# A two-layer transformer block on one core: q and k parts stored part-major and gathered in runs of neighbouring rows, and the first row maxima issued earlier

## The chip, the cores and the metric

The kernel runs on one NeuronCore of one Trainium2 chip. The metric is device microseconds of one launch. The kernel before has a median of 708.69 us over three runs (708.49, 708.69 and 711.36).

## The reference, cut to what matters

One sequence of 1024 tokens with 256 features passes two layers. Each layer has adaptive layer norms, an attention and an MLP, joined by gated residual updates.

Layer 0: a chunked linear attention with rotary embedding, then a gated MLP with 4-bit weights (2048 hidden features). Layer 1: causal softmax attention with 16 heads of 16 features and rotary embedding, then a second causal softmax attention of the same shape (no rotary embedding) inside the MLP branch, whose result modulates a gated MLP with 1024 hidden features.

```python
# layer 1, first attention (the second has no _rope and no biases)
q = _rope(proj(Wq, bq)); k = _rope(proj(Wk, bk)); v = proj(Wv, bv)
att = einsum('bhqd,bhkd->bhqk', q, k) / sqrt(16)
att = softmax(where(causal, att, -inf))
y = einsum('bhqk,bhkd->bhqd', att, v) @ Wo.T + bo
```

The change touches only the two softmax attentions, called "the first" (`l = 0` in `attention(l)`) and "the second" (`l = 1`) below.

## The kernel before, in words

The program is written out by engine; semaphores order the engines. TensorE computes projections, scores and products; VectorE and ScalarE move results out of PSUM; GpSimd (POOL) does small subtractions; the SP queue issues all DMAs.

Scores need more precision than bf16 gives, at bf16 speed. So q and k are each split in three bf16 parts (high, middle, low), and one matmul contracts over 96 rows: 16 features times six products of parts. For that, q and k stand in SBUF tiles `qr` and `kr`, [row, half of the tokens, head, token], where row 6*d + slot holds feature d of the part that belongs to the slot. Rows 96 to 98 of `qr` hold the row maxima, in three bf16 parts, and those of `kr` hold -1, so that a score comes out with its row maximum already subtracted.

The way of q and k in each attention: the projection lands feature-major in PSUM (in the first attention by way of rotary embedding on token-major tiles, L1179 to L1203, and transposes on TensorE, L697). `split` (ScalarE L923 to L940, VectorE L1216 to L1230, POOL `low_parts` L1611 to L1617) makes the three parts in pieces of 128 features by 512 tokens: `w` 0 to 3 are q and k of features 0 to 127 and 128 to 255 of the first token half, 4 to 7 those of the second half. `parts_out` (L395) stores a q piece and a k piece to a DRAM scratch `scr`, 384 KB each, and `spread` (L403) gathers them back with twelve DMAs of 128 KB, one for each slot of `qr` and of `kr`; it waits for both stores. The landing of one `spread(l, half, dt)` is counted in `qr_ld{2*half+dt}`.

Then the attention. There are eight blocks: four groups of four heads, for the first half of the queries (c = 0) and then for the second (c = 1). For each block there are banks of the row maxima (`max`: matmuls L742, mask L745, VectorE's maximum L1285), a `rowmax` step (POOL splits the maxima in three parts, TensorE transposes them at L751, ScalarE copies them to `m3T` at L973, and SP's `row_max` at L414 puts them into `qr` by a DMA), then per tile of 128 keys the scores (L768, mask L771), the exponential (ScalarE L962) and the product with v (L782). TensorE walks a list `ORDER`, computed once before the build by `attention_order()` from assumed costs; the same list serves both attentions, and ScalarE and VectorE walk it too. It starts with eleven banks of block 0, five of block 1, `rowmax` of block 0, six more banks of block 1, the first bank of block 2, and then the first score of block 0. Ahead of that first score TensorE runs six matmuls whose result nobody reads (`idle(6, 4)`, L760, executed at L471), and waits for the -1 rows and for the row maxima of block 0. A ring of three PSUM banks serves the maxima. In the second attention ScalarE waits ahead of the exponentials of the second step until the last stores of the second token half have landed (L956), since the tile `pt` shares memory with their source.

The order on the SP queue is written out at L421 to L434: store and gather of the first two pieces, then of the next two, the first store of the second half (`parts_out(l, 1, 0)`), `row_max(l, 0)`, the other store of the second half, its gathers and the other row maxima.

Of the kernel before, what the change touches and what calls it, by code (L numbers as in the profile page):

```python
# [186 lines left out]
def build(nc, a, out):  # L187
# [13 lines left out]
    with ctx:  # L201
# [59 lines left out]
        def piece(l, n, half):  # L261
# [54 lines left out]
        scr = nc.dram_tensor("parts_scratch", [4, P, 3, T], BF16, kind="Internal").ap()  # L316
# [10 lines left out]
            qt sp_h sp_r sp_m sp_l sp_p pw0 pw1 pw2 pw3 qr_ld0 qr_ld1 qr_ld2 qr_ld3 vp_e  # L327
# [3 lines left out]
            dq w_sc wf_h wf_l g_m u_m gl_s it_s it_h it_l fdn out_done""".split()  # L331
        names += [f"nat{i}" for i in range(FC[1])] + [f"ld_scale{i}" for i in range(4)]
# [10 lines left out]
        def _(sp):  # L343
# [77 lines left out]
            for l in range(2):  # L421
                parts_out(l, 0, 0)
                spread(l, 0, 0)
                parts_out(l, 0, 1)
                spread(l, 0, 1)
                parts_out(l, 1, 0)
                row_max(l, 0)
                parts_out(l, 1, 1)
                spread(l, 1, 0)
                row_max(l, 1)  # L430
                row_max(l, 2)
                spread(l, 1, 1)
                for blk in range(3, len(BLOCKS)):
                    row_max(l, blk)  # L434
# [15 lines left out]
        def _(pe):  # L450
# [260 lines left out]
            def attention(l):  # L711
# [19 lines left out]
                for what, i, *at in ORDER:  # L731
                    if what == "max":
                        blk, g, c, qt, ch, w, h0, k = BANKS[i]
                        if (g // 2, c) not in loaded:
                            loaded.append((g // 2, c))
                            pe.wait_ge(S[f"qr_ld{2 * c + g // 2}"], 16 * 12 * (l + 1))
# [17 lines left out]
                    elif what == "score":  # L754
# [111 lines left out]
        def _(act):  # L866
            def weight_hi(i, dst, off):
                if i == 0:
                    act.wait_ge(S["ld_raw0"], 80)
                elif i == 5:  # L870
                    act.wait_ge(S["ld_raw1"], 64)
                    act.wait_ge(S["vj"], 8)
                elif i == 9:
                    act.wait_ge(S["ld_raw2"], 64)
                    act.wait_ge(S["pw1"], 32)
                    act.wait_ge(S["pw3"], 32)
# [46 lines left out]
            def split(l, first=0, last=8):  # L923
                def middle(w):
                    act.wait_ge(S["sp_r"], 8 * l + w + 1)
                    half, n = divmod(w, 4)
                    act.copy(piece(l, n, half)[:, (1, 2)[n % 2], :], rest[:, w % 4, :]
                             ).then_inc(S["sp_m"], 1)

                for w in range(first, last + 1):  # L930
                    if w < last:
                        half, n = divmod(w, 4)
                        act.wait_ge(S["qt"], 8 * l + w + 1)
                        if l == 1 and w == 0:
                            for i in range(4):
                                act.wait_ge(S[f"pw{i}"], 32)
                        act.copy(piece(l, n, half)[:, (0, 1)[n % 2], :], bank[w % 4][:, :]
# [10 lines left out]
            def attention(l):  # L948
                act.activation(sd[:, 0:1], minus1[:, :], ACT.Exp)
                for what, i, *at in ORDER:  # L950
                    if what == "score":
# [3 lines left out]
                        if l == 1 and i == 1 and at[0] == 0:  # L955
                            act.wait_ge(S["pw3"], 64)  # L956
# [135 lines left out]
        def _(ve_):  # L1092
# [80 lines left out]
            def pairs(ap, l, i):  # L1173
# [3 lines left out]
                return ap.rearrange("p (h two j) -> p h two j", h=2 * H, two=2)[:, :, i, :]  # L1177

            def rope_cos(l, t):  # L1179
                dve.wait_ge(S["pj"], 8 * l + t + 1)  # L1180
                if t >= 2:
                    dve.wait_ge(S["rp_add"], 8 * l + t - 1)
                dve.tensor_tensor(t1[:, t % 2, :].rearrange("p (h d) -> p h d", d=DH),
                                  bank[4 + 2 * (t % 2)][:, :].rearrange("p (h d) -> p h d", d=DH),
                                  rope_c[:, l, t, :].unsqueeze(1).to_broadcast([P, 2 * H, DH]), ALU.mult
                                  ).then_inc(S["rp_t1"], 1)

            def rope_sin(l, t):
# [3 lines left out]
                for i in range(2):  # L1192
                    z = pairs(t2[:, t % 2, :], l, i), pairs(bank[4 + 2 * (t % 2)][:, :], l, 1 - i)
                    s = rope_s[:, l, t, :].rearrange("p (j two) -> p two j" if l == 0 else "p (two j) -> p two j", two=2)[:, i, :]
                    q = dve.tensor_tensor(z[0], z[1], s.unsqueeze(1).to_broadcast([P, 2 * H, DH // 2]), ALU.mult)
# [20 lines left out]
            def split(l, first=0, last=8):  # L1216
                for w in range(first, last + 1):
                    if w < last:
                        half, n = divmod(w, 4)
                        dve.wait_ge(S["sp_h"], 8 * l + w + 1)  # L1220
                        if w >= 4:
                            dve.wait_ge(*low_part(l, w - 4))
                        dve.tensor_tensor(rest[:, w % 4, :], bank[w % 4][:, :],
                                          piece(l, n, half)[:, (0, 1)[n % 2], :], ALU.subtract
                                          ).then_inc(S["sp_r"], 1)
                    if first < w <= 2:
# [3 lines left out]
                                          piece(l, n, half)[:, (1, 2)[n % 2], :], ALU.subtract).then_inc(S["sp_l"], 1)  # L1230
# [19 lines left out]
            def low_rank_halves():  # L1250
# [7 lines left out]
                for i in range(4):  # L1258
                    dve.wait_ge(S[f"pw{i}"], 64)
# [257 lines left out]
        def _(pool):  # L1517
# [93 lines left out]
            def low_parts(l):  # L1611

                for w in range(2, 8):
# [3 lines left out]
                                       piece(l, n, half)[:, (1, 2)[n % 2], :], ALU.subtract).then_inc(S["sp_p"], 1)  # L1617
# [83 lines left out]
```

## Time and profile before

| | |
|---|---|
| median of three runs | 708.69 us |
| profiled execution | 708.0 us |
| its span, first to last instruction | 706.1 us |
| TensorE busy | 654.3 us (93%) |
| VectorE busy | 457.2 us (65%) |
| ScalarE busy | 334.4 us (47%) |
| POOL busy | 149.7 us (21%) |
| mean granted TensorE clock | 0.988 of full |
| gathers into `qr` and `kr` | 96 DMAs of 128 KB |
| stores to the scratch | 16 DMAs of 384 KB |

Busy times of TensorE overlap with each other at their ends, because matmuls are pipelined. All dates in the rows are microseconds from the start of the span. The first attention begins its row maxima at 289.41, the second at 478.14.

### The profile page before, as it was taken

To read this page: it belongs to the slowest core of one execution; us is meant where nothing else is said; L and a number is where in the kernel's file an instruction comes from. 1 tells how busy PE (TensorE), PEld (TensorE's weight loads), DVE (VectorE), ACT (ScalarE), POOL (GpSimd) and SP (SyncE) were. 2 spreads that over 40 slices of the span, in tenths; PEclk is the share of its full clock that TensorE was granted. 3 is DMA by queue.
4 is the path that set the end of the run, shared out by engine and by line. 5 is a ranking of instruction groups with operands and counts; after the bars stand their busy time and mean duration, and the time that the engine had idled before them with its cause. 6 is when DMAs were issued, how large, how long until landed. Compare 5 with 4: busy or idle time off the path is not lost.

```text
span 706.1 us, 10697 instructions
## 1 busy us (share of the span) xinstructions
PE 654.3 (93%) x3990; PEld 405.8 (57%) x3990; DVE 457.2 (65%) x970; ACT 334.4 (47%) x531; POOL 149.7 (21%) x194
## 2 busy tenths in 40 slices
PE   4999979999999879899999998897999999999996
PEld 3667647777777656455444434483554444368884
DVE  5668787777777388778888602557788886242223
ACT  5334243333333423345567684561564657843332
POOL 3002224555555601310000000031100001003331
PEclk9999799999999999999999999999999999999999
DMA  7602410000000002663000000037410000050001
GB/s 263 227 0 91 128 44 0 24 23 22 1 0 1 0 1 75 190 186 92 2 2 2 1 2 1 1 125 227 137 54 2 2 2 2 20 160 1 1 0 59
DMA packets 36415, 38.34 MB, mean 54 GB/s; under 512 B 4034, under 2 KB 35292, under 8 KB 36108
## 3 DMA queue, kind: packets, MB, share of 16 engines
q1 hardware_dynamic: 36364, 37.67, 17.0%
q8 instruction: 31, 0.51, 0.3%
q14 instruction: 20, 0.16, 0.1%
HBM read 30.11 MB, written 7.34 MB: 53 GB/s over the span
## 4 chain that ended last, share of the span: by engine, by line
PE 47%; issue 22%; POOL 12%; DVE 11%; ACT 3%; DMA 2%; SPq 2%; POOLq 0%; DVEq 0%; ACTq 0%
POOL it_lo L1602 9%; PE psum L782 9%; PE psum L742 8%; PE psum L768 8%; PE psum L454 4%; DVE m L1285 3%; PE psum L455 3%; PE psum L456 3%; POOL wd L1581 2%; PE psum L771 2%; PE psum L745 2%; PE psum L471 2%; PE psum L570 1%; DVE mx L1285 1%; SPq L345 1%
## 5 line engine op out<-in xcount | busy, mean ns | idle before, releaser
L962 ACT ACTIVATE pt<-psum 128x1024 f32<-128x1024 f32 (+1 forms) x192 | 148.1, 811 | 93.2 <-PE psum L771 65.1
L1285 DVE TENSOR_REDUCE mx<-psum 128x1 f32<-128x512 f32 (+3 forms) x216 | 132.4, 665 | 16.3 <-PE psum L742 8.3
L742 PE MATMUL psum<-kr,qr 96*128 96x512 bf16 (+3 forms) x384 | 108.6, 332 | 5.7 <-DVE m L1285 2.7
L768 PE MATMUL psum<-qr,kr 99*128 99x512 bf16 (+3 forms) x384 | 97.6, 327 | 1.5 <-ACT pt L962 1.3
L1602 POOL TENSOR_TENSOR it_lo<-it,it_hi 128x512 fp32r<-128x512 f32 x48 | 67.3, 1402 | 146.2 <-ACT it_hi L1006 144.6
L782 PE MATMUL psum<-pt,vp 128*32 128x512 f32 (+3 forms) x768 | 81.7, 498 | 0.0
L454 PE MATMUL psum<-h_hi,wf_hi 128*128 128x512 f32 x192 | 75.4, 393 | 1.7 <-issue 1.7
L742 PEld LDWEIGHTS psum<-kr,qr 96*128 96x128 bf16 x384 | 36.3, 98 | 68.0 <-DVE mx L1285 29.4
L1006 ACT CAST it_hi<-it 128x512 fp32r<-128x512 f32 x48 | 29.9, 623 | 95.7 <-DVE it L1360 95.7
L455 PE MATMUL psum<-h_lo,wf_hi 128*128 128x512 f32 x192 | 74.8, 390 | 0.0
L456 PE MATMUL psum<-h_hi,wf_lo 128*128 128x512 f32 x192 | 74.8, 389 | 0.0
L1285 DVE TENSOR_REDUCE m<-psum 128x1 f32<-128x384 f32 (+3 forms) x88 | 50.6, 636 | 20.2 <-PE psum L745 19.9
L1360 DVE TENSOR_TENSOR it<-psum,gl 128x512 f32<-128x512 f32 x48 | 32.9, 685 | 43.0 <-PE psum L456 39.7
L768 PEld LDWEIGHTS psum<-qr,kr 99*128 99x128 bf16 x384 | 35.4, 98 | 41.3 <-ACT pt L962 23.0
L771 PE MATMUL psum<-identb,tri 128*128 128x128 bf16 x256 | 50.3, 219 | 0.0
L745 PE MATMUL psum<-tri,identb 128*128 128x128 bf16 x256 | 50.2, 224 | 0.0
L1630 POOL TENSOR_SCALAR m<-m 128x16 bf16<-128x16 f32 x16 | 4.1, 254 | 213.1 <-DVE m L1289 153.9
L454 PE MATMUL psum<-it_hi,wf_hi 128*128 128x512 f32 x96 | 39.4, 411 | 7.3 <-POOL it_lo L1602 7.3
L454 PEld LDWEIGHTS psum<-h_hi,wf_hi 128*128 128x128 f32 x192 | 36.1, 188 | 10.2 <-issue 2.5
L455 PEld LDWEIGHTS psum<-h_lo,wf_hi 128*128 128x128 f32 x192 | 36.1, 188 | 7.8 <-issue 0.2
L456 PEld LDWEIGHTS psum<-h_hi,wf_lo 128*128 128x128 f32 x192 | 36.0, 188 | 7.7
L1002 ACT ACTIVATE gl<-psum 128x512 f32<-128x512 f32 x48 | 28.6, 596 | 24.6 <-PE psum L533 16.4
(201 smaller groups left out, 1087.1 us busy)
## 6 DMA issues: line engine op xcount, KB each, us to landing
qr<-parts_scratch SPq DMA_DIRECT2D x48, 128.0 KB, 2.7
kr<-parts_scratch SPq DMA_DIRECT2D x48, 128.0 KB, 2.6
parts_scratch<-parts SPq DMA_DIRECT2D x12, 384.0 KB, 3.2
wmod<-in_L_wmod SPq DMA_DIRECT2D x1, 1536.0 KB, 6.3
parts_scratch<-qr SPq DMA_DIRECT2D x4, 384.0 KB, 3.2
x<-in_L_attn_x SPq DMA_DIRECT2D x2, 512.0 KB, 4.3
wmod<-in_L_wmod SPq DMA_DIRECT2D x1, 1024.0 KB, 5.3
packed<-in_L_ffn_gate_W_packed SPq DMA_DIRECT2D x1, 1024.0 KB, 7.2
```

The source lines that it names most:

```text
L454: pe.matmul(dst, st_hi, mv_hi, start=first, stop=False)
L455: pe.matmul(dst, st_hi, mv_lo, start=False, stop=False)
L456: return pe.matmul(dst, st_lo, mv_hi, start=False, stop=last)
L742: m = pe.matmul(b, qr[0:PARTS_ROWS, c, h, (qt - 4 * c) * P:(qt - 4 * c + 1) * P], kr[0:PARTS_ROWS, ch, h, 0:w], start=True, stop=not diag)
L745: m = pe.matmul(b[:, w - P:w], identb[:, :], tri[:, :], start=False, stop=True)
L768: m = pe.matmul(bank[4 + 2 * at[0] + j][:, 0:w], kr[0:PARTS_ROWS + 3, kt // 4, h, (kt % 4) * P:(kt % 4 + 1) * P], qr[0:PARTS_ROWS + 3, c, ...
L771: m = pe.matmul(bank[4 + 2 * at[0] + j][:, 0:P], tri[:, :], identb[:, :], start=False, stop=True)
L782: m = pe.matmul(bank[3][32 * j:32 * j + 32, q0 - c * HALF:q0 - c * HALF + w], vp[:, kt, 4 * gp + j, :], pt[:, (n + j // 2) % 4, j % 2, 0:w ...
L962: act.activation(pt[:, n % 4, :, 0:w], psum[:, b:b + 2, 0:w], ACT.Exp, scale=0.25).then_inc(S["ex"], 1)
L1285: dve.tensor_reduce(dst, bank[at[0]][:, 0:k * w].rearrange("p (k w) -> p k w", k=k), AX, ALU.max).then_inc(S["p1_mx"], 1)
L1360: dve.tensor_tensor(it[:, N % 2, :], bank[5][:, :], gl[:, N % 2, :], ALU.mult).then_inc(S["it_s"], 1)
L1602: pool.tensor_tensor(it_lo[:, N % 2, :], it[:, N % 2, :], it_hi[:, N % 2, :].bitcast(F32), ALU.subtract).then_inc(S["it_l"], 1)
```

## The change

1. The scratch is [4, part, 128 features, tokens] instead of [4, 128 features, part, tokens].
2. Within each 128 features, q and k are ordered by feature and then by head (d, h) instead of (h, d). For that, the columns of the weights and the biases of q and k of both attentions are permuted on the host, and the rotary embedding of the first attention multiplies with a table that is repeated over eight heads along the innermost axis.
3. The parts of k are kept in the opposite order from q's (q high, middle, low; k low, middle, high). The 96 rows are now 16 * slot + feature, and the six products need, for q, parts 0, 1, 2, then 0, 1, then 0, and for k, parts 0, 1, 2, then 1, 2, then 2 of its own order. So each gathers with three DMAs, of 48, 32 and 16 rows, 384, 256 and 128 KB.
4. The stores of q and k have their own semaphores; the gathers of q wait for q's store alone.
5. `row_max(l, 0)` stands ahead of `parts_out(l, 1, 0)` on the SP queue.
6. The six idle matmuls ahead of the first score are gone.

```diff
-        scr = nc.dram_tensor("parts_scratch", [4, P, 3, T], BF16, kind="Internal").ap()
+        scr = nc.dram_tensor("parts_scratch", [4, 3, P, T], BF16, kind="Internal").ap()
...
-                    sp.dma_start(scr[w2, :, :, tok], piece(l, w2, half)).then_inc(S[f"pw{2 * half + dt}"], 16)
+                    sp.dma_start(scr[w2, :, :, tok].rearrange("s p t -> p s t"), piece(l, w2, half)).then_inc(S[f"{'qk'[is_k]}w{2 * half + dt}"], 16)
...
-                sp.wait_ge(S[f"pw{2 * half + dt}"], 32 * (l + 1))
-                for is_k, (dst, order) in enumerate([(qr, (0, 1, 0, 1, 0, 2)), (kr, (1, 1, 2, 2, 0, 1))]):
-                    for slot, part in enumerate(order):
-                        sp.dma_start(dst[slot:PARTS_ROWS:6, half, 8 * dt:8 * dt + 8, :],
-                                     scr[2 * dt + is_k, :, part, tok].rearrange("(h d) t -> d h t", d=DH)
+                for is_k, dst in enumerate((qr, kr)):
+                    sp.wait_ge(S[f"{'qk'[is_k]}w{2 * half + dt}"], 16 * (l + 1))
+                    for first, part, n in ((0, 0, 3), (3, is_k, 2), (5, 2 * is_k, 1)):
+                        src = scr[2 * dt + is_k, part:part + n].rearrange("s (d h) t -> (s d) h t", d=DH)
+                        sp.dma_start(dst[DH * first:DH * (first + n), half, 8 * dt:8 * dt + 8, :], src[:, :, tok]
                                      ).then_inc(S[f"qr_ld{2 * half + dt}"], 16)
...
+                row_max(l, 0)
                 parts_out(l, 1, 0)
-                row_max(l, 0)
                 parts_out(l, 1, 1)
...
-                            pe.wait_ge(S[f"qr_ld{2 * c + g // 2}"], 16 * 12 * (l + 1))
+                            pe.wait_ge(S[f"qr_ld{2 * c + g // 2}"], 16 * 6 * (l + 1))
...
                             if blk == 0:
-                                idle(6, 4)
                                 pe.wait_ge(S["kr_ones"], 4)
...
-                return ap.rearrange("p (h two j) -> p h two j", h=2 * H, two=2)[:, :, i, :]
+                return ap.rearrange("p (g two j h) -> p g two j h", g=4, two=2, h=8)[:, :, i, :, :]
...
+                    z = [v.rearrange("p (g d h) -> p g d h", g=4, h=8) for v in (t1[:, t % 2, :], bank[4 + 2 * (t % 2)][:, :])]
+                    c = rope_c[:, l, t, :].unsqueeze(1).unsqueeze(3).to_broadcast([P, 4, DH, 8])
...
+                        s = s.unsqueeze(1).unsqueeze(3).to_broadcast([P, 4, DH // 2, 8])
```

The rest of the diff follows from these: the indices of the parts in `split`, the waits that named the old store semaphores (L875, L876, L936, L956, L1259), and the permutations on the host.

## Rows read from the trace of the kernel before

**Rows 1.** The page's clock line: 40 slices of 17.65 us, in tenths of full speed.
```profile
PEclk9999799999999999999999999999999999999999
```

**Rows 2.** Windows: stretch, us, busy time (instructions) by engine, clock, DMA share, GB/s.
```profile
303.00:325.00 22.00, 22.00 (x198) 11.70 (x197) 16.28 (x30) 11.70 (x20) 2.38 (x11) 1.00 0.57 168
478.00:479.00 1.00, 0.86 (x13) 0.87 (x14) 0.20 (x1) 0.99 (x2) 0.00 (x0) 1.00 1.04 358
493.00:494.00 1.00, 1.00 (x4) 0.41 (x3) 0.00 (x0) 0.00 (x0) 0.00 (x0) 0.51 1.00 350
```

**Rows 3.** TensorE's timeline, first attention: start, us, engine, line, operation, count, idle before.
```profile
287.67 1.90 PE L471 MATMUL psum<-spin,identb 128*128 128x512 bf16 x8 [1.02 <-DVE xn L1223]
289.41 0.22 PE L742 MATMUL psum<-kr,qr 96*128 96x128 bf16 x1
...
302.13 1.81 PE L471 MATMUL psum<-spin,identb 128*128 128x512 bf16 x6
303.78 0.38 PE L768 MATMUL psum<-qr,kr 99*128 99x512 bf16 x1
```

**Rows 4.** Waits, 289 to 320 and then 477 to 510 us: total, times, longest.
```profile
PEld psum L742 <- DMA kr<-parts_scratch: 0.5, 1, 0.5
...
PE psum L742 <- DMA kr<-parts_scratch: 0.9, 1, 0.9
```

**Rows 5.** TensorE's timeline, second attention.
```profile
478.14 0.22 PE L742 MATMUL psum<-kr,qr 96*128 96x128 bf16 x1 [0.93 <-DMA kr<-parts_scratch]
...
490.52 0.27 PE L742 MATMUL psum<-kr,qr 96*128 96x128 bf16 x1 [0.71 <-DVE m L1285]
...
491.33 2.77 PE L471 MATMUL psum<-spin,identb 128*128 128x512 bf16 x6
493.89 0.43 PE L768 MATMUL psum<-qr,kr 99*128 99x512 bf16 x1
```

**Rows 6.** Timeline of the SP queue, second attention.
```profile
464.11 1.94 SPq L401 DMA_DIRECT2D parts_scratch<-parts  x2
...
484.09 4.43 SPq L410 DMA_DIRECT2D kr<-parts_scratch  x6
...
489.88 0.79 SPq L418 DMA_DIRECT2D qr<-m3T  x1
490.71 1.57 SPq L401 DMA_DIRECT2D parts_scratch<-parts  x2
```

**Rows 7.** The page's DMA issues: count, KB each, median us from issue to landing.
```profile
kr<-parts_scratch SPq DMA_DIRECT2D x48, 128.0 KB, 2.6
parts_scratch<-parts SPq DMA_DIRECT2D x12, 384.0 KB, 3.2
```

**Rows 8.** VectorE's timeline at 489 us.
```profile
489.22 1.28 DVE L1285 TENSOR_REDUCE m<-psum 128x1 f32<-128x512 f32 x2
```

**Rows 9.** Timeline of the SP queue, first attention.
```profile
295.15 3.81 SPq L410 DMA_DIRECT2D kr<-parts_scratch  x6
...
300.32 0.83 SPq L418 DMA_DIRECT2D qr<-m3T  x1
```

**Rows 10.** ScalarE's timeline, both attentions.
```profile
298.41 0.26 ACT L973 COPY m3T<-psum 48x128 bf16<-48x128 bf16 x1 [8.62 <-PE psum L751]
...
477.24 0.37 ACT L920 COPY vp<-psum 128x256 f32<-128x256 f32 x1 [0.34 <-PE psum L456]
...
487.13 0.26 ACT L973 COPY m3T<-psum 48x128 bf16<-48x128 bf16 x1 [8.00 <-PE psum L751]
494.69 1.02 ACT L962 ACTIVATE pt<-psum 128x1024 f32<-128x1024 f32 x1 [7.30 <-PE psum L771]
```

**Rows 11.** VectorE's groups by form up to 460 us: count, busy us, mean ns, idle before.
```profile
L1195 DVE TENSOR_TENSOR t<-psum,rope_s 128x256 f32<-128x256 f32 x32 | 12.0, 416 | 0.2
L1183 DVE TENSOR_TENSOR t<-psum,rope_c 128x512 f32<-128x512 f32 x16 | 11.0, 686 | 15.8 <-PE psum L482 15.8
L1415 DVE TENSOR_TENSOR xn<-psum,rc 128x256 f32<-128x256 f32 x8 | 3.4, 419 | 0.0
```

More of the change, by code:

```diff
@@ L331, in build @@
             dq w_sc wf_h wf_l g_m u_m gl_s it_s it_h it_l fdn out_done""".split()
+        names += [f"{z}w{i}" for z in "qk" for i in range(4)]
         names += [f"nat{i}" for i in range(FC[1])] + [f"ld_scale{i}" for i in range(4)]
@@ L926, in middle @@
                     half, n = divmod(w, 4)
-                    act.copy(piece(l, n, half)[:, (1, 2)[n % 2], :], rest[:, w % 4, :]
+                    act.copy(piece(l, n, half)[:, 1, :], rest[:, w % 4, :]
                              ).then_inc(S["sp_m"], 1)
@@ L935, in split @@
                             for i in range(4):
-                                act.wait_ge(S[f"pw{i}"], 32)
-                        act.copy(piece(l, n, half)[:, (0, 1)[n % 2], :], bank[w % 4][:, :]
+                                act.wait_ge(S[f"qw{i}"], 16)
+                                act.wait_ge(S[f"kw{i}"], 16)
+                        act.copy(piece(l, n, half)[:, (0, 2)[n % 2], :], bank[w % 4][:, :]
                                  ).then_inc(S["sp_h"], 1)
@@ L1182, in rope_cos @@
                     dve.wait_ge(S["rp_add"], 8 * l + t - 1)
[L1183 to L1186, printed above, removed]
+                if l == 0:
+                    z = [v.rearrange("p (h d) -> p h d", d=DH) for v in (t1[:, t % 2, :], bank[4 + 2 * (t % 2)][:, :])]
+                    c = rope_c[:, l, t, :].unsqueeze(1).to_broadcast([P, 2 * H, DH])
+                else:
+                    z = [v.rearrange("p (g d h) -> p g d h", g=4, h=8) for v in (t1[:, t % 2, :], bank[4 + 2 * (t % 2)][:, :])]
+                    c = rope_c[:, l, t, :].unsqueeze(1).unsqueeze(3).to_broadcast([P, 4, DH, 8])
+                dve.tensor_tensor(z[0], z[1], c, ALU.mult).then_inc(S["rp_t1"], 1)
             def rope_sin(l, t):
@@ L1194, in rope_sin @@
                     s = rope_s[:, l, t, :].rearrange("p (j two) -> p two j" if l == 0 else "p (two j) -> p two j", two=2)[:, i, :]
-                    q = dve.tensor_tensor(z[0], z[1], s.unsqueeze(1).to_broadcast([P, 2 * H, DH // 2]), ALU.mult)
+                    if l == 0:
+                        s = s.unsqueeze(1).to_broadcast([P, 2 * H, DH // 2])
+                    else:
+                        s = s.unsqueeze(1).unsqueeze(3).to_broadcast([P, 4, DH // 2, 8])
+                    q = dve.tensor_tensor(z[0], z[1], s, ALU.mult)
                 q.then_inc(S["rp_t2"], 1)
@@ L1223, in split @@
                         dve.tensor_tensor(rest[:, w % 4, :], bank[w % 4][:, :],
-                                          piece(l, n, half)[:, (0, 1)[n % 2], :], ALU.subtract
+                                          piece(l, n, half)[:, (0, 2)[n % 2], :], ALU.subtract
                                           ).then_inc(S["sp_r"], 1)
@@ L1229, in split @@
                         dve.tensor_tensor(piece(l, n, half)[:, (2, 0)[n % 2], :], rest[:, (w - 1) % 4, :],
-                                          piece(l, n, half)[:, (1, 2)[n % 2], :], ALU.subtract).then_inc(S["sp_l"], 1)
+                                          piece(l, n, half)[:, 1, :], ALU.subtract).then_inc(S["sp_l"], 1)
             def scaled_product(u, w, f_sem, ok_sem, ok_base):
@@ L1258, in low_rank_halves @@
                 for i in range(4):
-                    dve.wait_ge(S[f"pw{i}"], 64)
+                    dve.wait_ge(S[f"qw{i}"], 32)
+                    dve.wait_ge(S[f"kw{i}"], 32)
                 dve.tensor_copy(b_hi[0:96, :], b_raw[0:96, :]).then_inc(S["bst"], 1)
@@ L1616, in low_parts @@
                     pool.tensor_tensor(piece(l, n, half)[:, (2, 0)[n % 2], :], rest[:, w % 4, :],
-                                       piece(l, n, half)[:, (1, 2)[n % 2], :], ALU.subtract).then_inc(S["sp_p"], 1)
+                                       piece(l, n, half)[:, 1, :], ALU.subtract).then_inc(S["sp_p"], 1)
             def attention(l):
@@ L1691 @@
             inputs[n].reshape(FC[1], P, KC, P).transpose(0, 3, 2, 1).reshape(F1, D))
-    given["bias_rows"] = _np.concatenate([_np.array(inputs[n]) for n in (
-        "L0_attn_bq", "L0_attn_bk", "L0_attn_bv", "L0_attn_bg", "L1_attn_bq", "L1_attn_bk")])
+    spread = _np.arange(D).reshape(2, 8, DH).transpose(0, 2, 1).reshape(-1)
+    for n in ("L1_attn_Wq", "L1_attn_Wk", "L1_ffn_Wq", "L1_ffn_Wk"):
+        given[n] = _np.ascontiguousarray(given[n][:, spread])
+    given["bias_rows"] = _np.concatenate(
+        [_np.array(inputs[n]) for n in ("L0_attn_bq", "L0_attn_bk", "L0_attn_bv", "L0_attn_bg")]
+        + [_np.array(inputs[n])[spread] for n in ("L1_attn_bq", "L1_attn_bk")])
     for name, arr in [*given.items(), ("rope_cos", cos), ("rope_sin", sin)]:
```

9 lines of the change are left out of this document (5 added, 4 removed).

## The prediction, made before the changed kernel was run

> **What bounds the kernel now.** The page comes first: its clock line [rows 1] shows TensorE granted full speed or nearly, but for one slice far ahead of the attentions. A low stretch of 3 or 4 us does not show in a slice of 17.65, so the starts of the attentions need finer windows. Both attentions run the same list of steps, so I read them side by side in the timelines of TensorE, the SP queue and ScalarE, and then asked the waits what TensorE waits for there. The reader is to see three stretches in each attention. In the first, TensorE waits for the transfers that bring q and k. In the second it does the row maxima of the first two blocks at VectorE's pace. From the first score on, its matmuls stand end to end (it is busy 22.0 of the 22 us from 303 to 325 [rows 2]), and nothing behind has a fixed date: whatever moves the first score moves the end of the kernel by as much.
>
> Where do the transfers bind? In the first attention not at the start: eight idle matmuls run from 287.67 and the first maxima follow at 289.41, which is the spacing of the idles and no more [rows 3]. In the second, TensorE waits 0.9 us for kr, and starts at 478.14 [rows 4, 5]. The next load binds again: the third block's first matmul stands at 490.52, 0.71 us after the one before it. The last of the twelve SP issues of that load started about 487.9 (484.09 + 4.43, less the 0.6 of one issue) and a landing takes 2.6, which gives 490.5 [rows 5 to 7]. The wait is put down to VectorE, but the bank it needs was free earlier: the reduces at 489.22 are two of 0.64, so the first was done by 489.9 [rows 8]. In the first attention only the weight load waited, 0.5 us, while the matmul had almost no gap [rows 4].
>
> Behind the third block's first bank come six idle matmuls, then the first score: 302.13 to 303.78 (1.65 us) and 491.33 to 493.89 (2.56 us) [rows 3, 5]. They cover the landing of the first block's row maxima, whose SP issue stands at 300.32 and 489.88, behind a second-half store [rows 6, 9].
>
> **The change part by part.** All terms are in the profiled execution (706.1 us span, 708.0 in all, 0.7 below the median of 708.7).
>
> *Six idle matmuls out, twice.* At full clock one takes 0.2175 us: eight fill 287.67 to 289.41 [rows 3]. Six are 1.3 us. At 1.2 GHz, the lower of the clock's two levels, they filled 2.56 us. The clock was at 0.51 in the slice 493 to 494 [rows 2], that is at the lower level until it returned just as the idles ended. How much of 2.56 is won depends on what runs there instead: real scores at half speed. They do by 493.9 what they would do in half that time, so at the end of the low stretch 1.3 us are won, not 2.56. The same holds for the 1.65. I take 1.3 + 1.3 = 2.6. Upper bound: 1.65 + 2.56 = 4.2, if the slow stretch costs the scores nothing (ScalarE's exponentials of 1.02 us would pace them anyway [rows 10]). Lower bound: the clock stays low longer, below.
>
> *Row maximum 0 issued ahead of the second-half store.* This is what makes the removal free. ScalarE has m3T at 298.41 + 0.26 = 298.67 [rows 10]; its issue can start there and takes 0.83 [rows 9]. Its landing is shown by no row. Bounds: from nothing to the 2.6 of a 128 KB piece, from the issue's start [rows 7]. With the larger it lands at 301.3, and TensorE comes for it at 302.13: no wait, 0.8 to spare. In the second attention the copy ends at 487.39 and TensorE comes 2.7 to 3.5 later, at 490.05 at the earliest with the four maxima matmuls and their masks of some 0.8 behind: no wait, 0.8 to spare. If it took as long as a 384 KB store, 3.2, it would still be in time. Queued behind the wait on SP are now the four second-half stores and all that follows. In the first attention the first pair goes out at about 299.5, after that issue, where before it went out just ahead of it; the second pair follows it directly. The gathers of that half then have half the issues, so they and row maximum 1 land earlier; but until 325 TensorE has no idle time in which an earlier landing could be won [rows 2]: nothing.
>
> *Twelve gathers of 128 KB become six (384, 256 and 128 KB, for q and k).* The SP queue issues one in 0.64 us: six in 3.81 [rows 9]. A 384 KB store takes as long to issue, two in 1.57 to 1.94 with their waits [rows 6], so I take 0.64 for the large gathers as well: 3.9 instead of 7.7 us. Bytes are the same, 1.5 MB; SP's pace gives 205 GB/s, and where transfers overlap 358 GB/s are reached [rows 2], at which 1.5 MB need 4.4 us. So a load lands 2.5 to 4 us earlier, and q's begin without waiting for k's store. That is more than the waits that can be won. Start of the second attention: behind the DMA stands ScalarE's last copy of v, done at 477.24 + 0.37 = 477.61 [rows 10], for which TensorE also waits; 478.14 becomes 477.7: 0.4 (bounds 0 and 0.9). Third block in the second attention: 490.52 becomes about 490.05, when the bank is free: 0.45 (0 to 0.7). Third block in the first: 0.1 (0 to 0.5). At the first attention's start nothing, the idles cover it.
>
> The row shows 358 GB/s for whatever partitions were written. The Trainium skill, "SBUF — State Buffer", section "Door 1: The DMA port swizzle", says that bandwidth depends on how many of 16 ports the written partitions reach, and that partitions 32 apart share one. By that, the new gather of 48 neighbouring partitions reaches eight ports, the old one of every sixth partition more. An estimate from that page (half the ports, so about half the rate) makes it some 8 us for a load; no run here shows it yet. A load that goes no faster is the third rival.
>
> *New store layout.* The stores write the same 1 KB runs, three parts 256 KB apart instead of 2 KB. In the second attention ScalarE's exponentials of the second step wait for the last of them (pt overlays its source). It was issued at 490.71 to 492.28 and would land 3.2 later [rows 6, 7]; now row maximum 0 leaves at 487.0 (the copy's 487.39 less the earlier start of 0.4), the four stores take 0.83 + 4 x 0.64 more, and the last lands by 493.0. The exponentials come about 493.9, an estimate: two pairs of scores and three banks with masks, 3.4 us at half clock, behind 490.5. Nothing, with 0.9 to spare.
>
> *Rope on the permuted features.* Same counts and sizes; the table is now repeated along the innermost axis. Such a repeat exists already: L1415, 128x256 from PSUM, takes 419 ns against 416 ns for L1195 [rows 11]. So nothing. A slower operation would be covered by VectorE's 15.8 us of idle before the sixteen L1183, about 1 us per tile. The transposes, matmuls, splits and host-side permutations keep their sizes: nothing.
>
> Sum: 2.6 + 0.4 + 0.45 + 0.1 = 3.55, say 3.6. 708.0 - 3.6 = 704.4; at the median's level 705.1. Bounds of the terms together: all upper ends, 4.2 + 0.9 + 0.7 + 0.5 = 6.3, gives 702.4; all lower ends but the clock's and the late maximum's, 2.6, gives 706.1.
>
> **The rivals.**
>
> *A wait takes the place of the idles.* Row maximum 0 lands when the idles would have ended. For: nothing shows its landing. Against: it now leaves 1.65 (first) and 2.5 us (second attention) earlier, and before it was in time for 303.78 after leaving at 300.32: 3.46 at most, and 298.67 + 3.46 = 302.13. If it took 4.1 us, TensorE would wait 0.65 in each attention: 1.3 of the 3.6 gone, 2.3 in all, 706.4.
>
> *The slow clock hides less.* The scores are paced by ScalarE while the clock is low, so that most of 4.2 comes out: 4.2 + 0.95 = 5.2, 703.5. For: an exponential takes 1.02 us, two scores with their masks at half clock 1.07. Against: banks of maxima stand between the scores.
>
> *The gathers go no faster*, bound by bytes or by where they are written: the change doesn't do what it says. The waits of 0.95 stay, 2.6 remain: 706.1. For: a gather now writes 48 neighbouring rows, where it wrote every sixth of 96. Against: a gather's data is small beside the 2.6 of its landing. Even at the old 7.7 us per load, begun when the first store has landed (464.11 + 3.2 = 467.3 [rows 6, 7]), the first would be in at 477.6, in time for 477.7.
>
> *Slower: the clock doesn't come back.* The place is the first scores of each attention. The idles depend on nothing and may be what brings the clock back; scores wait for ScalarE and VectorE. If the clock stayed low, each further microsecond would cost 0.5: from 3.6 / 0.5 = 7.2 us more at 1.2 GHz, in both attentions together, it decides against the change; 10 more in each cost 10, net +6.4, 715. Against: from the first score TensorE stood at 22.0 of 22 us at full clock, and at half speed the same work fills it more. The Trainium skill, "TensorE: Matmul & The Clock Gate", section "What's actually happening", has it that "the default state is throttled, and activity releases the throttle"; the trace agrees in that the clock was back at the end of the idles of 491.33 [rows 2, 5], and by that rule scores end to end should do as well. A second way to the same side, with its own chance, is a rope operation slower by half a microsecond and more per tile; at twice its time it is 0.69 + 2 x 0.42 = 1.5 more on eight tiles, of which 1.0 is hidden on the first five and nothing on the last three, which stand back to back behind the split of the first half: 2.5 + 4.5 = 7.0, net +3.4, 712.1.
>
> **How the numbers follow.** Forecast 50% (its own range 704.0 to 706.0), late maximum 14%, most of 4.2 comes out 12%, gathers no faster 12%, slower cases 12% (clock 6, rope 6). A measurement of this kernel can tell about 0.5% (3.5 us) from no change, so faster is below 705.15: that is half of the forecast's half (26%), the case of the slow clock hiding less (12%) and, for clock phases elsewhere that may move either way, some 6 more: 0.44. Slower than 712.2: most of the clock case and little of the rope case, some 0.07, and 0.02 for runs like the 711.4 of before: 0.09. The rest, 0.47, is within. Range 703.0 to 708.8: it leaves out the tail of the second case and the slower ones.
>
> **What would show it.** In the timelines after: six SP gathers per load in about 3.9 us; row maximum 0 leaving within 0.2 of ScalarE's copy; the first score of each attention within 0.2 of the last maxima matmul, at about 302.1 and 489 (all dates are 1.4 earlier there); the second attention starting within 0.2 of the last copy of v; L1183 and L1195 at 0.69 and 0.42. Wrong would be: a wait of TensorE on qr<-m3T, a granted clock of 0.5 beyond 4 us behind a first score, issues of 1 us and more for the large gathers, or first scores that move and an end that does not.

## The result, and the profile after

The changed kernel takes 713.66 us, median of 19 runs, against 709.74 us for the kernel before, 19 runs beside them: a ratio of 1.0057, 95% interval 1.0036 to 1.0078. It is slower by about 4 us where 3.6 us less was forecast, so the sign was wrong and the time lies outside the range. The forecast started from a median of 708.69 over three runs; over 19 runs that kernel stands 1.05 us higher, so part of the distance to the range (703.0 to 708.8) is a start that was too low. The profiled execution has a span of 711.9 us, 713.66 in all, against 706.1 and 708.0.

The page of the changed kernel first: the clock line, the DMA queue (packets, MB, time of the packets as a share of 16 engines' span), the start of the chain's shares and the DMA issues.

```profile
PEclk9999899999999999989999999996999999999999
...
q1 hardware_dynamic: 35596, 37.67, 21.6%
...
PE 45%; issue 22%; POOL 12%; DVE 9%; DMA 5%; ACT 3%; SPq 2%; POOLq 0%; DVEq 0%; ACTq 0%
...
qr<-parts_scratch SPq DMA_DIRECT2D x8, 384.0 KB, 5.3
kr<-parts_scratch SPq DMA_DIRECT2D x8, 384.0 KB, 7.6
...
parts_scratch<-parts SPq DMA_DIRECT2D x12, 384.0 KB, 3.3
```

The same line of the page of the kernel before:

```profile
q1 hardware_dynamic: 36364, 37.67, 17.0%
```

The bytes are the same, yet the packets took 21.6% of the span's engine time instead of 17.0%. A gather of k lands 7.6 us after its issue, where a piece of 128 KB took 2.6 [rows 7]. A 384 KB store lands after 3.3 us as before, so the size alone does not do it. The clock line now has a 6 in the slice from 480.5 to 498.3 us, the start of the second attention, where it had a 9 [rows 1].

TensorE's timeline after, both attentions (columns as in [rows 3]):

```profile
291.16 0.22 PE L743 MATMUL psum<-kr,qr 96*128 96x128 bf16 x1
...
303.88 0.63 PE L768 MATMUL psum<-qr,kr 99*128 99x512 bf16 x1
...
317.76 0.39 PE L768 MATMUL psum<-qr,kr 99*128 99x512 bf16 x1 [2.62 <-DMA qr<-m3T]
...
483.61 0.22 PE L743 MATMUL psum<-kr,qr 96*128 96x128 bf16 x1 [1.33 <-DMA kr<-parts_scratch]
...
496.12 0.29 PE L743 MATMUL psum<-kr,qr 96*128 96x128 bf16 x1
...
496.95 0.63 PE L768 MATMUL psum<-qr,kr 99*128 99x512 bf16 x1
...
510.04 0.39 PE L768 MATMUL psum<-qr,kr 99*128 99x512 bf16 x1 [1.12 <-DMA qr<-m3T]
```

The first score follows the first maxima by 12.72 us, where it was 14.37 [rows 3]; the idles did come out. But the stretch that was 22.0 of 22 us busy [rows 2] now holds a wait of 2.62 us for row maximum 1. Its counterpart in the second attention is 1.12 us. That attention starts with a wait of 1.33 for kr, which was 0.93 [rows 5].

The SP queue's timeline after says why; x2 and x3 are neighbouring issues put together:

```profile
290.93 1.86 SPq L412 DMA_DIRECT2D qr<-parts_scratch  x3
...
300.44 0.80 SPq L419 DMA_DIRECT2D qr<-m3T  x1
301.28 2.83 SPq L402 DMA_DIRECT2D parts_scratch<-parts  x4
...
307.32 1.91 SPq L412 DMA_DIRECT2D kr<-parts_scratch  x3
309.27 11.18 SPq L419 DMA_DIRECT2D qr<-m3T  x2
...
476.44 1.12 SPq L402 DMA_DIRECT2D parts_scratch<-qr  x2
484.45 1.86 SPq L412 DMA_DIRECT2D qr<-parts_scratch  x3
```

And the chain that ended last, after (start, us, what it waited in):

```profile
309.27 8.45 DMA qr<-m3T
...
476.44 7.99 DMA parts_scratch<-qr
...
487.65 8.42 DMA kr<-parts_scratch
...
502.15 7.84 DMA qr<-m3T
```

Four links of some 8 us. The first and last are a row maximum of some 12 KB issued right behind six gathers. The second is a store issued behind gathers, for which the next gathers wait until 484.45. The third is the last gather of a load: issued first at 484.45 and landed at 487.65 + 8.42 = 496.07, that load took 11.6 us.

To place the loss, I cut the execution where the same work is passed in each kernel: A is the time to TensorE's first maxima of the first attention, B from there to the second of ScalarE's copies of a block's result (`t<-psum`) in that attention, C to the first maxima of the second attention, D to its second such copy, E the rest. A is nearly all code that no experiment changed, and it spreads from 289.3 to 294.6 us over the profiles, in the main with how long the granted clock dips there. (In experiments 2 and 5, A also holds a wait for k of 1.27 and 3.06 us; in experiment 5 it is 299.56.) The changed kernel's 1.75 us more in A are there by 25.3 us, in layer 0, so its rope and first loads added none of them. So single profiles are compared by B + C + D, and the ratios of the timed runs decide. Dips fall into B, C and D too (C of experiments 9 and 11 has one at 431 to 435 us, that of the kernel before has none), so a difference of a microsecond or two between single profiles isn't firm. These sums are worked out from the timelines.

```
             A       B      C       D      B+C+D   against before
before     289.41  37.68  151.05  39.11   227.84
changed    291.16  40.98  151.47  39.27   231.72       +3.9
```

B + C + D gives 3.9, the timed medians 3.9, their ratio 4.0. Nearly all of it (3.3) is in B: 2.62 of waiting, some 1.7 more because the clock fell behind that wait, less 1.3 for the idles, which is 3.0. These windows after show the clock (columns as in [rows 2]):

```profile
315.00:318.00 3.00, 0.38 (x4) 0.12 (x3) 0.98 (x2) 0.00 (x0) 0.00 (x0) 1.00 0.50 81
318.00:321.00 3.00, 3.00 (x22) 1.30 (x21) 0.56 (x1) 2.46 (x4) 0.00 (x0) 0.64 0.00 0
321.00:324.00 3.00, 3.00 (x22) 1.58 (x24) 2.04 (x4) 1.59 (x3) 0.00 (x0) 0.79 0.71 148
```

At 0.64 and 0.79 of full speed, 3.0 us each do the work of 1.9 and 2.4: 1.7 lost. TensorE stood idle for 2.62 of the three microseconds before, still at full clock, and was busy all through these six. In experiment 3 below, a wait of 1.90 us at the same place was followed by a stretch at half clock as well; behind the 1.70 of experiment 4 the clock didn't fall.

In the second attention (D) three terms nearly cancel. The first score comes 13.34 us after the first maxima instead of 15.75, 2.4 less. The wait takes 1.12 of that. The rest goes to the clock: it stood at half from about 486 to 499.7 us, 13.6 us in all, where the kernel before had 3.4 us there and was back at full clock as its first score began. A window after, from the first score on, and one of the kernel before from its first score on:

```profile
497.00:500.00 3.00, 3.00 (x17) 1.82 (x15) 1.79 (x3) 1.02 (x1) 0.94 (x4) 0.54 1.02 313
```

```profile
494.00:495.00 1.00, 1.00 (x11) 0.72 (x10) 0.00 (x0) 0.31 (x1) 0.00 (x0) 1.00 0.98 268
```

At 0.54 of full speed the three microseconds do the work of 1.6: 1.4 lost. This is the 6 of the clock line.

### The profile page after: what moved, and what is told of

It reads as the page before. It is cut to its first block, busy times and chain, and to the rows that moved or that the text cites. A ratio compares the mean times of both kernels' runs of the same rounds, so it can differ in the third digit from the quotient of the medians.

```text
span 711.9 us, 10630 instructions
## 1 busy us (share of the span) xinstructions
PE 658.2 (92%) x3978; PEld 407.8 (57%) x3978; DVE 457.9 (64%) x970; ACT 334.6 (47%) x531; POOL 149.9 (21%) x194
## 3 DMA queue, kind: packets, MB, share of 16 engines
q1 hardware_dynamic: 35596, 37.67, 21.6%
## 4 chain that ended last, share of the span: by engine, by line
PE 45%; issue 22%; POOL 12%; DVE 9%; DMA 5%; ACT 3%; SPq 2%; POOLq 0%; DVEq 0%; ACTq 0%
POOL it_lo L1612 9%; PE psum L782 8%; PE psum L768 7%; PE psum L743 7%; PE psum L455 4%; PE psum L456 3%; PE psum L457 3%; DMA qr<-m3T 2%; POOL wd L1591 2%; PE psum L500 2%; PE psum L771 2%; PE psum L746 1%; DVE mx L1295 1%; DMA kr<-parts_scratch 1%; DVE x L1218 1%
## 5 line engine op out<-in xcount | busy, mean ns | idle before, releaser
L743 PE MATMUL psum<-kr,qr 96*128 96x512 bf16 (+3 forms) x384 | 112.6, 345 | 4.3 <-DMA kr<-parts_scratch 1.3
L768 PE MATMUL psum<-qr,kr 99*128 99x512 bf16 (+3 forms) x384 | 99.5, 332 | 5.3 <-DMA qr<-m3T 3.7
L746 PE MATMUL psum<-tri,identb 128*128 128x128 bf16 x256 | 52.8, 233 | 0.0
```

What stands on the lines that cost most here:

```text
L743: m = pe.matmul(b, qr[0:PARTS_ROWS, c, h, (qt - 4 * c) * P:(qt - 4 * c + 1) * P], kr[0:PARTS_ROWS, ch, h, 0:w], start=True, stop=not diag)
L746: m = pe.matmul(b[:, w - P:w], identb[:, :], tri[:, :], start=False, stop=True)
L768: m = pe.matmul(bank[4 + 2 * at[0] + j][:, 0:w], kr[0:PARTS_ROWS + 3, kt // 4, h, (kt % 4) * P:(kt % 4 + 1) * P], qr[0:PARTS_ROWS + 3, c, ...
```

## The experiments

All ratios are to the kernel before, run on the same chip, with 95% intervals. The chips' medians for that kernel were 710.44 to 710.47. The experiments rest on 12 runs each, experiment 2 on 6 and experiment 5 on 4. Where the number of gathers changes, so does the count of landings that TensorE waits for (2, 8 and 12; not shown below).

**1. The changed kernel, gathers onto every second row.** q's and k's rows are permuted alike, so products are the same.

```
+ row = {0: 0, 3: 1, 5: 2*2*DH + 1}[first]
- sp.dma_start(dst[DH*first : DH*(first+n), half, ...], ...)
+ sp.dma_start(dst[row : row + 2*DH*n - 1 : 2, half, ...], ...)
```

> The changed kernel with one edit: the gathers keep source, sizes (384, 256, 128 KB), count and order, but write every second row (0, 2, .. 94, then 1 .. 63, then 65 .. 95) instead of neighbouring rows. Theory A (destination: neighbouring rows crowd the writes): the 384 KB gathers land in about 3.5 to 4.5 us instead of 5.3 and 7.6, the DMA queue's share falls from 21.6% back to 17 to 18%, TensorE's waits on qr<-m3T (2.6 and 1.1 us) go, and the kernel comes out about 3 us below the kernel before, ratio about 0.995. Theory B (source: reads at the new pitch of the scratch are slow) and theory C (large gathers fill the DMA rings): nothing changes, landings 5 to 8 us, share 21%, ratio 1.006 as for the changed kernel.

Ratio 0.9983 [0.9955, 1.0012]. Same six gathers, same bytes and packet count, only the rows written differ. From its page:

```profile
q1 hardware_dynamic: 35596, 37.67, 18.5%
...
qr<-parts_scratch SPq DMA_DIRECT2D x8, 384.0 KB, 4.1
kr<-parts_scratch SPq DMA_DIRECT2D x8, 384.0 KB, 5.8
```

B + C + D is 223.96, 3.9 less than before and 7.8 less than changed. By the timed ratios it is worth 5.2 us (1.2 below before, within the error, against 4.0 above). The rows written are the cause of the slow gathers.

**2. The changed kernel, twelve gathers of sixteen neighbouring rows.**

```
- for first, part, n in ((0, 0, 3), (3, is_k, 2), (5, 2*is_k, 1)):
+ for first, part, n in ((0,0,1), (1,1,1), (2,2,1), (3,is_k,1), (4,is_k+1,1), (5,2*is_k,1)):
```

> The changed kernel with each gather of 48 or 32 rows cut into gathers of 16 neighbouring rows: again twelve of 128 KB for q and k together, same source layout, same destination rows. Theory C (size): landings return to about 2.7 us, share 17%, ratio about 0.995 to 1.0. Theory A (destination): each gather now writes fewer different places at once, so packets stay slow or get slower, share 21% or more, landings above 4 us, ratio 1.005 or more. Theory B (source): as for A in the landings, ratio 1.005.

Ratio 1.0284 [1.0239, 1.0329]. The page and the waits:

```profile
q1 hardware_dynamic: 36364, 37.67, 24.2%
...
kr<-parts_scratch SPq DMA_DIRECT2D x48, 128.0 KB, 6.4
```

```profile
PE psum L743 <- DMA kr<-parts_scratch: 12.2, 4, 4.7
```

With the sizes, count and packets of before but neighbouring rows, a 128 KB piece of k lands after 6.4 us, not 2.6, and TensorE waits 12.2 us for k. Small pieces of neighbouring rows are worse than large ones.

**3. The changed kernel, scratch rows 128 elements longer.**

```
- scr = nc.dram_tensor("parts_scratch", [4, 3, P, T], ...)
+ scr = nc.dram_tensor("parts_scratch", [4, 3, P, T + 128], ...)
```

> The changed kernel with a scratch whose rows are 1152 instead of 1024 tokens long, so that no pitch in it is a power of two; stores and gathers move the same bytes in the same runs of 1 KB. Theory B (source): gathers land in 3 to 4.5 us, share back to 17 to 18%, ratio about 0.995. Theories A and C: no change, share 21%, ratio about 1.006.

Ratio 1.0034 [1.0010, 1.0058], with an interval that overlaps the changed kernel's. The gathers land exactly as late:

```profile
qr<-parts_scratch SPq DMA_DIRECT2D x8, 384.0 KB, 5.3
kr<-parts_scratch SPq DMA_DIRECT2D x8, 384.0 KB, 7.6
```

The pitch of the source is not what makes them slow.

**4. The kernel before with only the order and the idles changed.**

```
+ row_max(l, 0)
  parts_out(l, 1, 0)
- row_max(l, 0)
  ...
- idle(6, 4)
```

> The kernel before with two edits only: row_max of block 0 ahead of the first second-half store, and the six idle matmuls ahead of the first score gone. Transfers as before. My prediction's term: 1.3 us for each of the two attentions, 2.6 in all, plus little for the gathers, ratio about 0.996, no wait of TensorE on qr<-m3T. Rival (the idles bring the clock back, or a late row maximum takes their place): the low stretch after the first score is longer than 4 us or TensorE waits, ratio 1.0 or above.

Ratio 1.0001 [0.9974, 1.0028]: no gain. Its TensorE timeline has what ate it, and its SP queue the cause:

```profile
317.15 0.39 PE L767 MATMUL psum<-qr,kr 99*128 99x512 bf16 x1 [1.70 <-DMA qr<-m3T]
```

```profile
310.94 3.81 SPq L410 DMA_DIRECT2D kr<-parts_scratch  x6
314.80 5.05 SPq L418 DMA_DIRECT2D qr<-m3T  x2
```

Row maximum 1 is issued at 314.80 and lands 2.31 us later, at 317.11; TensorE came for it at 315.45. In the kernel before the first score stands 14.37 us behind the first maxima, here 12.37; it comes that much later for the row maximum too, and doesn't wait. So the forecast's largest term was not free even with the old transfers.

**5. The kernel before with neighbouring rows.**

```
- sp.dma_start(dst[slot:PARTS_ROWS:6, half, ...], ...)
+ sp.dma_start(dst[DH*slot : DH*(slot+1), half, ...], ...)
```

> The kernel before with one edit: each of its gathers writes 16 neighbouring rows (16 * slot and on) instead of every sixth. Source layout, sizes, order, idles as before. Theory A (destination: neighbouring rows crowd the writes), which the runs so far favour (rows apart 0.998, twelve gathers of sixteen neighbouring rows 1.028): landings of 4.5 to 6.5 us instead of 2.7, DMA queue share about 24% instead of 17%, 15 to 20 us slower, ratio 1.02 to 1.03. Rival (it needs the new source layout too): ratio below 1.005 and landings of 2.7.

Ratio 1.0240 [1.0190, 1.0289]. One line of the kernel before, moving nothing but the destination rows, costs 17 us. The page, then one window in which gathers run, here and in the kernel before:

```profile
q1 hardware_dynamic: 36364, 37.67, 23.7%
...
kr<-parts_scratch SPq DMA_DIRECT2D x48, 128.0 KB, 6.9
```

```profile
303.00:309.00 6.00, 4.87 (x33) 1.90 (x31) 6.00 (x13) 0.02 (x1) 0.94 (x4) 0.99 1.11 169
```

```profile
292.00:298.00 6.00, 4.98 (x32) 1.91 (x32) 6.00 (x12) 0.00 (x0) 0.95 (x4) 1.00 0.64 180
```

The first moves 169 GB/s at a DMA share of 1.11, the second 180 GB/s at 0.64. The time of a packet grew, not the number of bytes.

**6. Experiment 4, and row maximum 1 issued between q's and k's gathers.**

```
  for is_k, ...:
+     if early and is_k:
+         row_max(l, 1)
```

> The kernel before with row_max of block 0 early and the idles gone (which came out at 1.000) and one more edit: row_max of block 1 stands between the q and the k gathers of the second half instead of behind both. Theory D (the 2.6 us of the idles were eaten by row maximum 1, queued behind twelve gathers: TensorE waited 1.7 and 0.2 us for it): these waits go, and the first stretch from the first maxima to the second block's end falls from 37.6 to about 35.9 us in the first attention; ratio about 0.996. Rival (the removal wins nothing because the slow clock holds the scores): waits go and the ratio stays at 1.000, with a low-clock stretch that grows.

Ratio 0.9963 [0.9935, 0.9991], 2.6 us below experiment 4, though the two intervals overlap a little. The SP queue and a wait of ScalarE:

```profile
310.35 0.78 SPq L420 DMA_DIRECT2D qr<-m3T  x1
311.17 3.78 SPq L412 DMA_DIRECT2D kr<-parts_scratch  x6
```

```profile
497.37 0.81 ACT L962 ACTIVATE pt<-psum 128x768 f32<-128x768 f32 x1 [1.97 <-DMA parts_scratch<-parts]
```

Issued 3.4 us earlier than in experiment 4, counted from the first maxima, the row maximum is no longer waited for, and the idles' removal pays. B + C + D is 225.49, 2.35 less than before; its second attention has no stretch at half clock at all, so not all of that need be the edit's. The second line shows the next wait in line: the exponentials over the source of the last store.

**7. Experiment 1 with the six idles back** (`+ idle(6, 4)`).

> The changed kernel with the gathers on every second row (0.998 before) and the six idle matmuls back ahead of each first score. My term says 1.3 us for each attention: ratio about 0.998 + 0.0037 = 1.002. Rival (idles cover waits or hold the clock up): no slower than without them, 0.998 or less.

Ratio 0.9976 [0.9947, 1.0004], not told from experiment 1's 0.9983. In the profiles B is 1.07 and D 1.20 longer with the idles, 2.3 of the 2.6 forecast. The timed runs do not show them, but intervals of 2 us either way could hide most of that.

**8. The changed kernel, every third row, eight gathers.**

```
- for first, part, n in ((0, 0, 3), (3, is_k, 2), (5, 2*is_k, 1)):
+ for row, step, part, n in ((0,3,0,2), (1,3,is_k,2), (2,6,2,1), (5,6,2*is_k,1)):
...
+     sp.dma_start(dst[row:PARTS_ROWS:step, half, ...], ...)
```

> The changed kernel with gathers that reach over all 96 rows as before: for each of q and k two of 256 KB on every third row and two of 128 KB on every sixth, eight per load instead of six or twelve. Theory A: landings of about 3 to 4 us, DMA queue share 17 to 17.5% (every second row: 18.5%), no wait of TensorE on a DMA, ratio 0.994 to 0.997, a little below every second row. Rival C (what counts is how many bytes are queued at once): landings 4 to 6 us as with every second row, same ratio 0.998.

Ratio 0.9943 [0.9914, 0.9972]: 706.66 us, below both kernels. Its DMA issues:

```profile
qr<-parts_scratch SPq DMA_DIRECT2D x16, 256.0 KB, 3.8
kr<-parts_scratch SPq DMA_DIRECT2D x16, 256.0 KB, 4.5
```

TensorE waits for no DMA at the row maxima, and B + C + D is 223.72, 4.1 less than before.

**9. The changed kernel with the six idles back** (`+ idle(6, 4)`).

> The changed kernel with the six idle matmuls back ahead of each first score, nothing else. Theory D (behind slow gathers row maximum 1 lands at a date that the idles do not move, so their removal won nothing here): same time as the changed kernel, ratio 1.005 to 1.006, TensorE's wait on qr<-m3T of 2.6 us about 1.3 to 1.6 us shorter. Rival (the idles' removal did win its 2.6 us and the rest of the change cost 6.6): ratio about 1.009, the wait unchanged.

Ratio 1.0063 [1.0032, 1.0094], no different from changed. TensorE's timeline:

```profile
318.11 0.39 PE L769 MATMUL psum<-qr,kr 99*128 99x512 bf16 x1 [0.71 <-DMA qr<-m3T]
...
509.52 0.39 PE L769 MATMUL psum<-qr,kr 99*128 99x512 bf16 x1 [1.14 <-DMA qr<-m3T]
```

In the first attention the wait is 1.9 shorter than the changed kernel's 2.62, by about the idles put back: a wait behind them takes what their removal gives.

**10. The changed kernel, row maximum 1 issued ahead of the gathers.**

```
+ row_max(l, 1)
  spread(l, 1, 0)
- row_max(l, 1)
```

> The changed kernel with row_max of block 1 ahead of the first gathers of the second half instead of behind them (the gathers begin about 5 us later); neighbouring rows as in the change. If the landing of row maximum 1 is the main cost in the first attention, the waits of 2.6 and 1.1 us and the low-clock stretch behind the first go: 4 us less, ratio about 1.000 to 1.001, with what is left in the later start of the second attention. If the slow gathers cost it by the loads themselves, TensorE now waits for kr of the second half at its block 4, and the ratio stays at 1.005 or above.

Ratio 0.9973 [0.9947, 1.0000]. Its SP queue:

```profile
308.66 0.76 SPq L419 DMA_DIRECT2D qr<-m3T  x1
309.47 1.91 SPq L412 DMA_DIRECT2D qr<-parts_scratch  x3
```

The slow gathers are all still there, and TensorE no longer waits for row maximum 1. The +4.0 us of the change becomes -1.9, with an interval that ends at no change: nearly 6 us against the changed kernel hang on the place of one small DMA.

**11. The kernel before without the idles, the order kept** (`- idle(6, 4)`).

> The kernel before with the six idle matmuls gone and nothing else: row maximum 0 still behind the first second-half store. Row maximum 0 leaves at 300.3 of the kernel before's dates and TensorE comes at 302.1: with a landing of 2.3 us (as row maximum 1 showed) TensorE waits about 0.5 us there, then 1.3 to 1.7 us for row maximum 1: ratio 1.000. Rival (row maximum 1 is only late because row maximum 0 went first): ratio 0.996.

Ratio 1.0047 [1.0022, 1.0073], not the 1.000 expected. TensorE's timeline, and windows behind the second wait:

```profile
305.08 0.58 PE L767 MATMUL psum<-qr,kr 99*128 99x512 bf16 x1 [1.43 <-DMA qr<-m3T]
...
498.22 0.58 PE L767 MATMUL psum<-qr,kr 99*128 99x512 bf16 x1 [1.52 <-DMA qr<-m3T]
```

```profile
498.00:501.00 3.00, 2.78 (x14) 1.71 (x15) 0.88 (x2) 1.02 (x1) 0.00 (x0) 0.50 0.95 294
501.00:504.00 3.00, 3.00 (x18) 1.65 (x17) 1.41 (x3) 1.87 (x3) 0.00 (x0) 0.67 0.69 206
```

The idles hid a landing of row maximum 0 of some 3.1 us (issued 301.87) behind the stores. The half clock began at about 493, ahead of the second wait, and lasted until about 503: 10.2 us, where the kernel before has 3.4 there. Without the earlier issue the removal costs 3.3 us; with it (experiment 4) nothing.

**12. Experiment 8, and row maximum 1 between q's and k's gathers** (the edit of 6).

> The third-rows version (0.9943, no wait of TensorE on a DMA) with row_max of block 1 between the q and the k gathers of the second half. No wait is left for it to remove: same ratio, 0.993 to 0.996. If it is below 0.992, something of that queue still bound.

Ratio 0.9946 [0.9917, 0.9976], the same as experiment 8. Where gathers land in 3.8 to 4.5 us the row maximum is in time in its old place. The B + C + D of 222.64 is a further 1.1 less, but from one profile each and not seen in the timing.

## Why the prediction was wrong, point by point

*Twelve gathers of 128 KB become six* is the step that failed. Its first half, the issue pace, held: three in 1.86 to 1.91 us. Its second half, "a load lands 2.5 to 4 us earlier", took 358 GB/s and a landing of 2.6 us from gathers onto every sixth row and stores, and applied them to gathers onto 48 neighbouring rows. These land in 5.3 and 7.6 us, and the load of the third block in the second attention took 11.6. The same load took some 10.3 in the kernel before (480.23 to 490.5), and 2.5 to 4 less was forecast. Experiment 5 shows it alone (1.024), experiment 1 takes it out (0.998), experiments 2 and 3 exclude the piece size and the source pitch. The port rule weighed in the prediction (the Trainium skill, "SBUF — State Buffer", section "Door 1: The DMA port swizzle") agrees in direction. By its partition table a gather onto sixteen neighbouring rows reaches four ports, and the queue took 23.7 to 24.2%. The changed kernel's gathers of 48, 32 and 16 rows reach eight, eight and four (21.6%). Experiment 1's reach sixteen, eight and eight, because rows 1 to 63 and rows 65 to 95 lie in one half of the table each (18.5%). Every sixth row reaches thirteen or fourteen (17.0%). The pieces of experiment 8 reach sixteen and thirteen or fourteen and took 17.8%, so the last two don't follow the order; their pieces also differ in size. The prediction's estimate from that page, some 8 us for a load, had the direction that its forecast lacked. That ports are the mechanism is argued; that neighbouring rows are the cause is shown. My reason against the rival, that a gather's data is small beside its landing, mistook data of one piece for that of twelve in flight.

The terms that hung on it turned round. Start of the second attention: 0.4 was to be won, and its wait for the first load became 1.33 instead of 0.93, 0.4 lost: the last gathers of k were issued by 476.40 and TensorE got them at 483.61. Third block of the second attention: 12.51 us behind the first maxima instead of 12.38, where 0.45 was to be won, because the store issued at 476.44 behind those gathers landed 8 us later and its own gathers were as slow.

*The gathers go no faster* named the cause but priced only the gains that would stay away (706.1). It left out that slower gathers delay what is queued behind them. That is the second error, in the step *Row maximum 0 issued ahead of the second-half store*: that the gathers "and row maximum 1 land earlier" was priced at nothing. It went out at 309.27 and landed 8.45 us later. I had read 22.0 of 22 us busy as room, and it said only that there was no wait. The margin of row maximum 1 was never worked out as that of row maximum 0 was. Experiment 4 shows that the margin was less than the idles removed, and experiment 10 that the change's loss, nearly 6 us against it, is this wait with its clock.

*Six idle matmuls out, twice* was sized right in the trace: 12.72 us instead of 14.37 in the first attention, and 1.07 and 1.20 in experiment 7 against 1. But it can be a gain only where nothing waits behind. In the timed runs, removing the idles gave nothing in experiment 4 and nothing from experiment 9 to the changed kernel; experiment 6 comes out 2.6 us below 4. Experiments 1 and 7, where nothing waits behind, should differ by it too and do not, within 2 to 3 us.

*Row maximum 0* itself was right: no wait on it in the changed kernel, and without the move experiment 11 pays 1.43 and 1.52. The first rival's mechanism, a wait in place of the idles, was right for the wrong row maximum. Of the slower case, "the clock doesn't come back", a piece happened twice: the clock fell behind a wait in the first attention, for 1.7 us of work, and was still at half for the first scores of the second attention, for 1.4. Whether the missing idles have a part in the second is open. There the profiles with idles have 3.4 us at half clock (before, 7) or none (9); those without have none (6), 3.4 (1, 8, 10, 12), 6.8 (3, 4), 10.2 (11) and 13.6 (the changed kernel), from one profile each; 2 and 5, with waits of 4.7 and 5.8 us for k at that start, are left out. *New store layout* cost nothing in the changed kernel, but its "0.9 to spare" was not there: where row maximum 1 no longer holds TensorE up, ScalarE waits for the last of these stores, 1.3 us in experiment 1, 0.2 in 8, 1.6 in 10, 0.8 in 12, and 2.0 in 6, which has the old layout. *Rope* cost nothing, as said, in the groups of VectorE:

```profile
L1204 DVE TENSOR_TENSOR t<-psum,rope_s x32: 406/415/429, 21.8 to 283.2; 128x256 f32<-128x256 f32 x32
```

That is 415 ns against 416 [rows 11].

What stays open: why every third row takes a little more engine time per byte than every sixth, what set the length of the half clock in the second attention, and whether experiment 8 is really faster than 1, since the intervals overlap and B + C + D differ by only 0.2 us.

## What to carry to other kernels

Before merging DMAs, compare which partitions each writes, not only their number and bytes: neighbouring rows made the same bytes slower here by more than the saved issues. A stretch in which an engine never waits says nothing of the margin; when something ahead of it is taken out, work out the landing of every transfer that it will come for, the small ones behind large ones first. Issue such a small DMA ahead of the bulk: moving one 12 KB transfer in front of six gathers turned 4.0 us lost into 1.9 won, with no change just within the error.

## What the runs showed of the hardware that was not expected

- Destination rows alone: 128 KB pieces onto sixteen neighbouring rows land in 6.9 us where every sixth row takes 2.6; DMA share 1.11 at 169 GB/s instead of 0.64 at 180.
- A 12 KB transfer issued behind 1.5 MB of such gathers landed 8.45 us later, behind the old ones 2.31.
- Spread rows and larger pieces together gave the lowest time: eight gathers onto every third row, 706.66 us, 0.9943 [0.9914, 0.9972] of the kernel before. The intervals of experiments 1, 6 and 10 overlap with it.
- A wait of TensorE of 2.62 us at full clock was followed by 0.64 and 0.79 over the next six microseconds, though TensorE was busy all through them.
- At the start of the second attention the clock stayed at half for 13.6 us in the changed kernel and for 3.4 in the kernel before, though TensorE waited for nothing from 488 to 500.
